# Two groups' weighted sums in one block on TensorE, and three units in another order, in a two-layer cross-attention kernel

## The chip, the cores and the metric

The kernel runs on one core of a Trainium2 chip. The metric is the device time in microseconds (us) from launch to end. A profile of one execution is read beside it; its times count from the start of its own span. TensorE (PE) multiplies and transposes, and loads weights (PEld) under running matmuls; VectorE (DVE), ScalarE (ACT) and GpSimd (POOL) work on what it leaves; SyncE (SP) issues most transfers.

## The reference

For each of 16 images `x` is 112 x 320 and its context 375 x 192. Two cross-attentions follow each other, the first with 8 heads of 40 over 371 context rows, with a small second attention over 4 token rows, the other with 20 heads of 16 over all 375 rows. Cut to what matters:

```python
hs = _mha(x @ Wq, enc @ Wk, enc @ Wv)                 # layer 0, 8 heads
ca_hs1 = _mha((ca.T @ Wq_ca)[:, indices, :], x, x)    # over the image's own 112 rows
ca_hs2 = _mha(ca_hs1 @ Wq, ca @ Wk_ca, ca @ Wv_ca)    # over 4 token rows
x1 = (hs + ca_hs2) @ Wout + b_out + x
q, k, v = heads(x1 @ Wq), heads(ctx @ Wk), heads(ctx @ Wv)   # layer 1, 20 heads
probs = softmax(q @ k.T / 4)
out = (probs @ v) @ Wo + bo + x1
```

## The kernel before

**Groups and iterations.** Heads are worked in groups of four: two groups per image in the first layer (layer 0), five in the second (layer 1). The program is a software pipeline of 18 iterations `t`, each of 7 slots `i`. In slots 0 and 1 the two layer-0 groups of image `t` are scored, in slots 2 to 6 the five layer-1 groups of image `t - 1`. (The last image's are one slot sooner.) In each slot TensorE, in this order, does: the first pair of heads' scores of this slot's group, units, the *shifted scores* of the group of two slots ago (scores again, keys on partitions, with the row maximum as one more row of the product), the transpose of the maxima of the group of one slot ago, units, the second pair's scores, units, the *attend* (probabilities times values) of the group of two slots ago, units. The four places for units are the phases 0 to 3 of `UNITS`, a table written by hand; beside each name stands the image's offset to `t`.

**Units.** K0, K1, V0, V1 are parts of the keys and values; q0 and q1 the queries; q0T and q1T their transposes; W2, S2_0, S2_1, T2_0, T2_1, PV2, S3, p3T the small attentions; N0, N1a, N1b transpose attend results back, and VectorE divides them by the sum of the probabilities (a reciprocal and a product); hn0T, hn1T, x1T transpose the inputs of the projections, out0 and out1 are the projections. All units take two PSUM banks, `bankX0` and `bankX1`, strictly in turn: a unit waits until the unit two places before it has been read out (`bank_drained`). For K0, K1, q0, q1 and the transposes of queries that is ScalarE's rounded copy and then VectorE's remainder or masked copy.

**Queues.** Each engine runs its own list in program order, slot by slot. ScalarE in a slot: phase 0 units, the exponentials of the group of two slots ago (`exps`), the DMA that places the maxima (`place_m`), phase 1, 2, 3 units. VectorE: the first pair's maximum, phase 0 units, the copy of the transposed maxima (`copy_mT`), phase 1 units, the second pair's maximum, phase 2 units, the copy of the attend's result (`copy_o`), phase 3 units.

**Banks.** `bankS` (two banks, one for each head of a pair) holds scores until VectorE has their maximum; `bankST` the shifted scores; `bankO` the attend results and, in its first columns, the transposed maxima `bank_mT`. So before the change a transpose of maxima waits until the attend result has been copied (`o_copied`), and an attend until the maxima have (`mT_copied`). An attend is 12 matmuls: layer 1 puts four heads on four column groups of 32, layer 0 two heads on two column groups of 64. The trace counts each of these fp32 matmuls twice.

Of the kernel before, what the change touches and what calls it, by code (L numbers as in the profile page):

```python
# [11 lines left out]
B, SQ, HID = 16, 112, 320  # L12
SK, CAD, NTOK = 375, 192, 4
# [71 lines left out]
GROUPS = list(SCORED.values())  # L85
NUMBER = {g: n for n, g in enumerate(GROUPS)}


# [23 lines left out]
def xattn_kernel(nc, xT, xpad, ctxT, caS, caT, w_all, w_ca, wqT, bd96, consts, bias, out):  # L112
    g_rows = nc.dram_tensor("g_rows", [B, 3, 32, HID], F32, kind="Internal").ap()

    with ExitStack() as ctx:
# [436 lines left out]
        def _(act):  # L552
# [46 lines left out]
            def unit(name, b):  # L599
# [27 lines left out]
                elif kind == "V0":  # L627
                    if i == 0 and b == 0:
                        act.wait_ge(zeroed, 3)
                    elif i == 0:  # L630
                        act.wait_ge(pv_done, NUMBER[0, b - 1, 1] + 1)
                    nc.scalar.activation(v0[0:KC, i, :].rearrange("p (h d) -> p h d", h=H0)[:, :, 0:D0],
                                         X[0:KC, 0:HID].rearrange("p (h d) -> p h d", h=H0), ACT.Copy)\
                        .then_inc(free, 1)
                elif kind == "V1":
                    if i == 0 and b < 2:
                        act.wait_ge(zeroed, 6 + b)
                    elif i == 0:
                        act.wait_ge(pv_done, NUMBER[1, b - 2, G1 - 1] + 1)
                    nc.scalar.activation(v1[b % 2][0:KC, i, :].rearrange("p (h d) -> p h d", h=H1)[:, :, 0:D1],  # L640
# [90 lines left out]
        def _(dve):  # L731
# [48 lines left out]

            def copy_o(g):
                layer, b, k = g
                n = NUMBER[g]
                dve.wait_ge(pv_done, n + 1)
                if layer == 0:
                    dst, src = o0T[:, 2 * k:2 * k + 2, :].rearrange("p c q -> p (c q)"), bankO[:, 0:2 * SQ]
                else:
                    at = (2 + n % 2) * SQ
                    dst, src = o1T[:, k, :], bankO[:, at:at + SQ]
                nc.vector.tensor_copy(dst, src).then_inc(o_copied, 1)  # L790
# [119 lines left out]
            for t in ITERATIONS:  # L910
                for i in range(SLOTS):
                    g, before, late = scored_at(t, i), scored_at(t, i, 1), scored_at(t, i, LAG)
                    if g:
# [13 lines left out]
                    for u in units_of(t, i, 2):  # L927
                        unit(*u)
                    if late:
                        copy_o(late)  # L930
                    for u in units_of(t, i, 3):
# [14 lines left out]
        def _(pe):  # L946
# [61 lines left out]
            def unit(name, b):  # L1008
# [80 lines left out]
                elif kind in ("N0", "N1a", "N1b"):  # L1089
                    layer, k = {"N0": (0, 1), "N1a": (1, 3), "N1b": (1, 4)}[kind]  # L1090
                    pe.wait_ge(o_copied, NUMBER[layer, b, k] + 1)
                    cols = [o0T[:, c, :] for c in range(4)] if layer == 0 else [
# [43 lines left out]

            def scores(g, pair):
                layer, b, k = g
# [59 lines left out]

            def attend(g, transposed):
                layer, b, k = g  # L1200
                n = NUMBER[g]
                pe.wait_ge(exp_done, n + 1)
                pe.wait_ge(mT_copied, transposed)
                if n > 0:
                    pe.wait_ge(o_copied, n)
                if k == 0:
                    for i in range(NKC):
                        pe.wait_ge(bank_drained[bank(f"V{layer}_{i}", b)], drained(f"V{layer}_{i}", b))
                src = PT[:, n % 2]
                if layer == 0:  # L1210
                    at_once = [(c, j) for pair in range(2) for c in range(NKC) for j in (2 * pair, 2 * pair + 1)]
                else:
                    at_once = [(c, j) for c in range(NKC) for j in range(GROUP)]
                for c, j in at_once:
                    h = GROUP * k + j
                    if layer == 0:
                        keys = KC if c < 2 else KC - NTOK
                        dst = bankO[64 * (j % 2):64 * (j % 2) + 64, (j // 2) * SQ:(j // 2 + 1) * SQ]
                        v = v0[0:keys, c, 64 * h:64 * h + 64]
                    else:  # L1220
                        keys = KC
                        at = (2 + n % 2) * SQ
                        dst = bankO[32 * j:32 * j + 32, at:at + SQ]
                        v = v1[b % 2][0:keys, c, 32 * h:32 * h + 32]
                    last = nc.tensor.matmul(dst, v, src[0:keys, c, SQ * j:SQ * j + SQ], start=(c == 0),  # L1225
                                            stop=(c == NKC - 1))
                last.then_inc(pv_done, 1)
# [16 lines left out]

            attended = transposed = 0
            for t in ITERATIONS:
                for i in range(SLOTS):
                    g, before, late = scored_at(t, i), scored_at(t, i, 1), scored_at(t, i, LAG)
                    if g:
                        scores(g, 0)  # L1250
                    for u in units_of(t, i, 0):
                        unit(*u)
                    if late:
                        shifted_scores(late)
                    if before:
                        transpose_m(before, attended)
                        transposed = NUMBER[before] + 1
                    for u in units_of(t, i, 1):
                        unit(*u)
                    if g:  # L1260
                        scores(g, 1)
                    for u in units_of(t, i, 2):
                        unit(*u)
                    if late:
# [79 lines left out]
```

## Time and profile before

| | before |
|---|---|
| median of three runs | 755.55 us (755.02 to 756.1) |
| profiled execution's own time | 753.38 us |
| its span | 751.5 us |
| TensorE matmul, busy | 703.0 us (94%) |
| TensorE weight load, busy | 610.3 us (81%) |
| VectorE, busy | 472.3 us (63%) |
| ScalarE, busy | 404.0 us (54%) |
| GpSimd, busy | 295.5 us (39%) |
| mean granted TensorE clock | 0.983 |

"Busy" is the union of an engine's instructions. A record `[0.33 <-ACT arena L595]` behind a row of the timeline says that the engine sat idle 0.33 us before it, and which work ended that. The chain of work that ended last follows, back from the end, what released each step; 69% of it is TensorE's. Names such as `L1225` are lines of the kernel: L1159 and L1156 are scores, L1193 and L1187 shifted scores, L1172 the transpose of maxima, L1225 the attend, L1095 the transposes of N0, N1a and N1b, L1111 the S2 units, L1105 W2, L1071 and L1078 query transposes, L1087 the transposes hn0T, hn1T and x1T, L1005 keys, values, queries and projections.

### The profile page before, as it was taken

What the parts mean: (1) busy time and instruction counts of PE and PEld (TensorE: products, weight loads), DVE (VectorE), ACT (ScalarE), POOL (GpSimd) and SP (SyncE); (2) the same over time, 40 slices, a digit from 0 to 9 for tenths busy, and PEclk for the clock granted to TensorE, in tenths of its full rate; (3) what the DMA queues carried; (4) which work ended last, traced back from release to release, by engine and by line L of the source; (5) the groups of instructions that cost most, each with busy time, mean ns of one, the idle gap of its engine ahead of it and who ended that gap; (6) DMA issues with size and microseconds to landing.
All of it is one profiled execution on the core that took longest, in us unless ns stands there. A gap on an engine that the chain in (4) does not pass through costs nothing.

```text
span 751.5 us, 18194 instructions
## 1 busy us (share of the span) xinstructions
PE 703.0 (94%) x6924; PEld 610.3 (81%) x6924; DVE 472.3 (63%) x1028; ACT 404.0 (54%) x923; POOL 295.5 (39%) x401
## 2 busy tenths in 40 slices
PE   8787999999999999999999999999999999999975
PEld 5586888888888888888888888888888888888763
DVE  2653666657576665757576575756667575766662
ACT  2454555555565555565555555556555555654432
POOL 5485662444334253433325344323524542330300
PEclk9889999999999999999999999999999999999996
DMA  9533553443516244252524434261533425051400
GB/s 325 175 96 96 112 133 75 107 80 79 133 47 143 62 119 95 67 118 54 137 60 125 92 80 103 62 142 45 136 81 94 89 76 129 20 137 28 87 7 11
DMA packets 52387, 72.45 MB, mean 96 GB/s; under 512 B 12128, under 2 KB 44256, under 8 KB 52304
## 3 DMA queue, kind: packets, MB, share of 16 engines
q1 hardware_dynamic: 44832, 60.34, 31.7%
q0 software_dynamic: 6144, 9.25, 6.5%
q10 hardware_dynamic: 1328, 1.71, 0.6%
q8 instruction: 57, 0.93, 0.5%
q14 instruction: 26, 0.21, 0.1%
HBM read 20.60 MB, written 4.26 MB: 33 GB/s over the span
## 4 chain that ended last, share of the span: by engine, by line
PE 69%; ACT 13%; DVE 8%; issue 3%; POOL 1%; DMA 1%; SPq 1%; ACTq 0%; POOLq 0%
PE bankX L1005 28%; PE bankO L1225 8%; PE bankST L1193 7%; ACT arena L577 7%; PE bankS L1159 6%; PE bankST L1187 5%; ACT arena L595 3%; DVE negmax L773 2%; DVE q1T L829 2%; PE bankX L1118 2%; PE bankX L1125 2%; PE bankX L1087 2%; PE bankS L1156 2%; ACT q1T L666 2%; PE bankX L1071 2%
## 5 line engine op out<-in xcount | busy, mean ns | idle before, releaser
L773 DVE TENSOR_REDUCE negmax<-bankS 112x2 f32<-112x750 f32 (+1 forms) x224 | 208.7, 932 | 57.0 <-PE bankS L1159 32.7
L494 POOL DMA_DIRECT2D k_stack<-stage x192 | 96.6, 511 | 181.5 <-DVE stage L809 153.9
L577 ACT ACTIVATE arena<-bankST 125x1344 f32<-125x1344 f32 x80 | 103.5, 1294 | 30.9 <-PE bankST L1193 30.9
L1225 PE MATMUL bankO<-arena,v 125*32 125x112 f32 (+2 forms) x2688 | 107.2, 264 | 6.2 <-ACT arena L577 4.4
L1225 PEld LDWEIGHTS bankO<-arena,v 125*32 125x32 f32 (+2 forms) x2688 | 81.2, 117 | 29.0 <-issue 12.7
L1159 PE MATMUL bankS<-k_stack,q1T 112*112 112x376 f32 x320 | 87.8, 355 | 4.1 <-DVE negmax L773 3.0
L1005 PE MATMUL bankX<-ctx_hi,WH 128*120 128x376 f32 (+2 forms) x192 | 69.0, 360 | 3.0 <-DVE qn L765 2.2
L457 POOL TENSOR_TENSOR w2bd<-w2s,cst 96x896 fp32r<-96x896 f32 x16 | 29.9, 1870 | 98.4 <-DVE w2s L765 98.4
L1005 PE MATMUL bankX<-WH,ctx_hi 128*125 128x320 f32 x192 | 66.1, 344 | 0.1
L1193 PE MATMUL bankST<-q1T,k_stack 112*125 112x224 f32 x480 | 65.4, 272 | 0.0
L1005 PE MATMUL bankX<-ctx_hi,WL 128*120 128x376 f32 (+2 forms) x192 | 64.0, 334 | 0.0
L1193 PEld LDWEIGHTS bankST<-q1T,k_stack 112*125 112x125 f32 x480 | 62.0, 188 | 0.8 <-DMA q1T<-mT 0.4
L1005 PE MATMUL bankX<-WL,ctx_hi 128*125 128x320 f32 x192 | 58.5, 312 | 0.0
L1159 PEld LDWEIGHTS bankS<-k_stack,q1T 112*112 112x112 f32 x320 | 49.4, 177 | 8.8 <-DVE negmax L773 6.5
L829 DVE TENSOR_SCALAR q1T<-bankX,odd_rows 128x448 fp32r<-128x448 f32 (+1 forms) x48 | 29.1, 606 | 41.7 <-ACT q1T L666 41.2
L595 ACT ACTIVATE arena<-bankX,negmax 112x112 f32<-112x112 f32 x128 | 43.6, 354 | 21.7 <-DVE negmax L837 21.6
L1005 PE MATMUL bankX<-WH,act_hi 128*112 128x320 f32 x144 | 46.7, 325 | 3.3 <-DVE act_hi L866 1.4
L483 POOL TENSOR_TENSOR xb<-xp,bias_sb 112x320 f32<-112x320 f32 x16 | 13.9, 867 | 88.7 <-DVE x L860 88.6
L779 DVE CAST mT<-bankO 4x112 fp32r<-4x112 f32 x112 | 29.0, 259 | 30.0 <-PE bankO L1172 30.0
L1187 PEld LDWEIGHTS bankST<-q0T,k_stack 121*125 121x125 f32 (+1 forms) x384 | 46.0, 187 | 0.0
L619 ACT ACTIVATE stage<-bankX 128x376 fp32r<-128x376 f32 (+1 forms) x48 | 23.1, 482 | 41.7 <-PE bankX L1005 41.0
L1187 PE MATMUL bankST<-q0T,k_stack 121*125 121x112 f32 (+1 forms) x384 | 44.9, 266 | 0.0
(141 smaller groups left out, 1545.8 us busy)
## 6 DMA issues: line engine op xcount, KB each, us to landing
k_stack<-stage SPq DMA_DIRECT2D x96, 176.2 KB
k_stack<-stage SPq DMA_DIRECT2D x192, 70.5 KB, 2.6
k_stack<-stage POOLq DMA_DIRECT2D x192, 47.0 KB, 2.0
ctx_raw<-in_ctxT SPq DMA_DIRECT2D x16, 376.0 KB, 3.3
k_stack<-stage SPq DMA_DIRECT2D x48, 117.5 KB
xp<-in_xpad SPq DMA_DIRECT2D x16, 224.0 KB, 3.3
x_raw<-in_xT SPq DMA_DIRECT2D x16, 168.0 KB, 2.4
out<-x1b SPq DMA_DIRECT2D x16, 140.0 KB, 3.2
```

The costliest lines, as they stand in the source:

```text
L457: nc.gpsimd.tensor_tensor(w2bd[:, :, :], w2s[:, :].bitcast(F32).unsqueeze(1).broadcast_to((96, H0, SQ)), mask96.unsqueeze(2).broadcast_to( ...
L494: pool.dma_start(dst, src).then_inc(k1_stacked_pool[b % 2], 16)
L577: nc.scalar.activation(dst[0:KC], bankST[0:KC, :, 0:GROUP * SQ], ACT.Exp).then_inc(exp_done, 1)
L595: last = nc.scalar.activation(prob2[0:SQ, h, :], X[0:SQ, (h % 4) * SQ:(h % 4 + 1) * SQ], ACT.Exp, bias=negmax2[:, h:h + 1], accum_out=sum2 ...
L773: nc.vector.tensor_reduce(negmax[:, n % 2, 2 * pair:2 * pair + 2], bankS[0:SQ, :, 0:keys], axis=AX, op=ALU.max, negate=True).then_inc(max_ ...
L779: nc.vector.tensor_copy(mT[:, n % MT_BUFS, :], bank_mT).then_inc(mT_copied, 1)
L829: nc.vector.tensor_scalar(q1T[:, 4 * i:4 * i + g, 1, :], X[:, 0:g * SQ].rearrange("p (h q) -> p h q", h=g), odd_rows[:, :], None, ALU.mult ...
L1005: last = nc.tensor.matmul(dst, lhs, rhs, start=(n == 0), stop=(n == len(passes) - 1))
L1159: last = nc.tensor.matmul(bankS[0:SQ, j, 0:SKP], q1T[0:ROWS1, h // 2, h % 2, :], k1_stack[b % 2][0:ROWS1, h // 2, :], start=True, stop=True)
L1187: last = nc.tensor.matmul(bankST[0:keys, c, SQ * j:SQ * j + SQ], k0_stack[0:M_ROW0 + 1, h, KC * c:KC * c + keys], q0T[0:M_ROW0 + 1, h, :], ...
L1193: last = nc.tensor.matmul(bankST[0:KC, c, 2 * SQ * pair:2 * SQ * pair + 2 * SQ], k1_stack[b % 2][0:ROWS1, 2 * k + pair, KC * c:KC * c + KC ...
L1225: last = nc.tensor.matmul(dst, v, src[0:keys, c, SQ * j:SQ * j + SQ], start=(c == 0), stop=(c == NKC - 1))
```

## The change

Attends are done by *episodes*: the two layer-0 groups in one block, in the slot of the second (slot 3), the layer-1 groups 0 and 1 in slot 5, 2 and 3 in slot 0 of the next iteration, and 4 alone in slot 1. The other slots (2, 4, 6) have no attend. `pv_done` and `o_copied` count episodes. The transposed maxima move from `bankO` to free columns of the second bank of `bankS`; their transpose now waits for the first maximum of this slot's group, since VectorE reads that bank, and the second head's scores wait until the maxima are copied. In the table, N1a ("four groups' transposes") moves from slot 1 phase 3 to phase 1, between q1T_2 and q0; in slot 4 out1 moves to phase 1, and p3T and N0 to phase 2.

```diff
-    ([("q1T_1", -1), ("V1_2", -1)], [("q1T_2", -1)], [("q0", 1)], [("N1a", -2), ("K1_0", 0)]),
+    ([("q1T_1", -1), ("V1_2", -1)], [("q1T_2", -1), ("N1a", -2)], [("q0", 1)], [("K1_0", 0)]),
...
-    ([("K0_2", 1)], [("p3T", 0), ("N0", 0)], [("out1", -2)], [("q0T_0", 1)]),
+    ([("K0_2", 1)], [("out1", -2)], [("p3T", 0), ("N0", 0)], [("q0T_0", 1)]),
...
+EPISODES = [e for b in range(B + 1) for e in
+            ([[(0, b, 0), (0, b, 1)]] if b < B else []) +
+            ([[(1, b - 1, 0), (1, b - 1, 1)], [(1, b - 1, 2), (1, b - 1, 3)], [(1, b - 1, 4)]] if b > 0 else [])]
+EPISODE = {g: n for n, e in enumerate(EPISODES) for g in e}
+def attended_at(t, i):
+    late = scored_at(t, i, LAG)
+    return EPISODES[EPISODE[late]] if late and EPISODES[EPISODE[late]][-1] == late else None
...
-        bank_mT = bankO[0:GROUP, 0:SQ]
+        bank_mT = bankS[0:GROUP, 1, SKP + 8:SKP + 8 + SQ]
...
-                    act.wait_ge(pv_done, n - 1)
+                    act.wait_ge(pv_done, EPISODE[GROUPS[n - 2]] + 1)
...
                 for j in range(2):
                     h = GROUP * k + 2 * pair + j
+                    if j == 1 and transposed > 0:
+                        pe.wait_ge(mT_copied, transposed)
...
-            def transpose_m(g, attended):
+            def transpose_m(g, scoring):
                 n = NUMBER[g]
-                pe.wait_ge(max_done, 2 * n + 2)
+                if scoring:
+                    pe.wait_ge(max_done, 2 * NUMBER[scoring] + 1)
+                else:
+                    pe.wait_ge(max_done, 2 * n + 2)
                 if n > 0:
                     pe.wait_ge(mT_copied, n)
-                else:
-                    pe.wait_ge(g_split, 4)
-                if attended > 0:
-                    pe.wait_ge(o_copied, attended)
...
-            def attend(g, transposed):
+            def attend(groups):
+                n = EPISODE[groups[0]]
                 if n > 0:
                     pe.wait_ge(o_copied, n)
+                for g in groups:
+                    layer, b, k = g
+                    pe.wait_ge(exp_done, NUMBER[g] + 1)
...
-                    if late:
-                        attend(late, transposed)
-                        attended = NUMBER[late] + 1
+                    if attended_at(t, i):
+                        attend(attended_at(t, i))
```

VectorE's `copy_o` copies an episode at once (448 columns in layer 0, 224 or 112 in layer 1), in `attended_at`'s slots.

The rows below are TensorE's list in a middle iteration. First slot 1, before: q1T_2's second transpose, the second pair's scores, the first and last of q0's eight matmuls, the attend of group 4, N1a (`o1T`) and the first matmul of K1_0.

```order
L1078 MATMUL bankX<-cst,qn 128x112
L1156 MATMUL bankS<-k_stack,q0T 112x372 [waits max_done]
L1156 MATMUL bankS<-k_stack,q0T 112x372
L1005 MATMUL bankX<-WH,x_hi 112x320 [waits x_split,bank_drained1]
...
L1225 MATMUL bankO<-arena,v_1 32x112 [waits o_copied,mT_copied,exp_done]
L1225 MATMUL bankO<-arena,v_1 32x112 x11
L1095 MATMUL bankX<-cst,o1T 112x128 [waits o_copied,bank_drained0]
L1095 MATMUL bankX<-cst,o1T 112x128 x3
L1005 MATMUL bankX<-ctx_hi,WH 128x376 [waits bank_drained1]
```

The same place of the changed kernel:

```order
L1090 MATMUL bankX<-cst,qn 128x112
L1107 MATMUL bankX<-cst,o1T 112x128 [waits o_copied,bank_drained1]
L1107 MATMUL bankX<-cst,o1T 112x128 x3
L1170 MATMUL bankS<-k_stack,q0T 112x372 [waits max_done]
L1170 MATMUL bankS<-k_stack,q0T 112x372 [waits mT_copied]
L1017 MATMUL bankX<-WH,x_hi 112x320 [waits x_split,bank_drained0]
...
L1241 MATMUL bankO<-arena,v_1 32x112 [waits exp_done,o_copied]
L1241 MATMUL bankO<-arena,v_1 32x112 x11
L1017 MATMUL bankX<-ctx_hi,WH 128x376 [waits bank_drained1]
```

N1a has gone ahead of the scores, and q0 has changed banks: it follows q1T_2 in bank 0, where it followed V1_2 in bank 1.

Slot 2, before, from S2_0 (`w2bd`) to S2_1, with N1b and the attend of layer 0's first group between:

```order
L1111 MATMUL bankX<-w2bd,ca_st 112x448 [waits w2_expanded,ca_split,bank_drained0]
L1159 MATMUL bankS<-k_stack,q1T 112x376 [waits max_done]
L1159 MATMUL bankS<-k_stack,q1T 112x376
L1095 MATMUL bankX<-cst,o1T 112x128 [waits o_copied,bank_drained1]
L1225 MATMUL bankO<-arena,v 64x112 [waits bank_drained0,bank_drained1,o_copied,mT_copied,exp_done]
L1225 MATMUL bankO<-arena,v 64x112 x11
L1111 MATMUL bankX<-w2bd,ca_st 112x448 [waits bank_drained0]
```

The same place of the changed kernel:

```order
L1123 MATMUL bankX<-w2bd,ca_st 112x448 [waits w2_expanded,ca_split,bank_drained0]
L1173 MATMUL bankS<-k_stack,q1T 112x376 [waits max_done]
L1173 MATMUL bankS<-k_stack,q1T 112x376 [waits mT_copied]
L1107 MATMUL bankX<-cst,o1T 112x128 [waits o_copied,bank_drained1]
L1123 MATMUL bankX<-w2bd,ca_st 112x448 [waits bank_drained0]
```

The attend is gone from between the two S2 halves, which share a bank; its twelve matmuls stand in slot 3 now.

Slot 4 of the changed kernel, from the transpose of the maxima to hn0T of slot 5 (before, p3T and N0 stood behind the transpose, and out1 and an attend behind the second pair's scores):

```order
L1185 MATMUL bankS<-cst,negmax 4x112 [waits mT_copied,max_done]
L1017 MATMUL bankX<-WH,act_hi 112x320 [waits bank_drained1,bank_drained0]
...
L1173 MATMUL bankS<-k_stack,q1T 112x376 [waits max_done]
L1173 MATMUL bankS<-k_stack,q1T 112x376 [waits mT_copied]
L1110 MATMUL bankX<-cst,p3w 96x112 [waits p3_split,bank_drained1]
L1107 MATMUL bankX<-cst,o0T 112x128 [waits o_copied,bank_drained0]
L1107 MATMUL bankX<-cst,o0T 112x128 x3
L1083 MATMUL bankX<-cst,qn 120x112 [waits bank_drained0,bank_drained1]
...
L1099 MATMUL bankX<-cst,hn 128x112 [waits bank_drained0]
```

N0 now takes the bank of out1, two places before it, and only q0T_0 and the next slot's scores stand between N0 and hn0T.

## Rows read from the trace of the kernel before

**Rows 1.** The page's granted TensorE clock, in 40 slices of the span.

```profile
PEclk9889999999999999999999999999999999999996
```

**Rows 2.** Timeline, slot 1: start us, duration us, engine, line, operation [idle before].

```profile
337.62 1.29 ACT L577 ACTIVATE arena<-bankST 125x1344 f32<-125x1344 f32 x1 [0.21 <-PE bankST L1193]
...
337.72 0.57 PE L1156 MATMUL bankS<-k_stack,q0T 120*112 120x372 f32 x2
...
338.13 0.31 PE L1005 MATMUL bankX<-WH,x_hi 128*112 128x320 f32 x1
...
338.81 0.34 ACT L666 ACTIVATE q1T<-bankX 64x224 fp32r<-64x224 f32 x1
...
339.18 0.45 DVE L829 TENSOR_SCALAR q1T<-bankX,odd_rows 128x224 fp32r<-128x224 f32 x1 [1.21 <-ACT q1T L666]
...
340.93 0.45 PE L1005 MATMUL bankX<-ctx_hi,WH 128*128 128x376 f32 x1 [0.17 <-DVE qn L765]
...
341.90 0.51 PE L1159 MATMUL bankS<-k_stack,q1T 112*112 112x376 f32 x2
```

**Rows 3.** Timeline, slots 2 and 3, and S2_1 one iteration later.

```profile
345.17 0.44 PE L1111 MATMUL bankX<-w2bd,ca_st 96*112 96x448 f32 x1
...
347.86 0.46 PE L1111 MATMUL bankX<-w2bd,ca_st 96*112 96x448 f32 x1 [0.33 <-ACT arena L595]
...
352.28 1.38 PE L1225 MATMUL bankO<-arena,v 125*64 125x112 f32 x24
...
353.59 0.43 PE L1005 MATMUL bankX<-ctx_hi,WH 128*120 128x376 f32 x1
...
391.19 0.46 PE L1111 MATMUL bankX<-w2bd,ca_st 96*112 96x448 f32 x1 [0.29 <-ACT arena L595]
```

**Rows 4.** The chain that ended last: start us, us on the chain, what.

```profile
346.35 1.46 ACT arena L595 x8
...
369.83 1.17 PE bankX L1005 x8
371.00 0.71 PE bankO L1225 x24
```

**Rows 5.** Timeline, slots 4 and 5.

```profile
355.83 0.93 DVE L773 TENSOR_REDUCE negmax<-bankS 112x2 f32<-112x750 f32 x1
...
356.42 0.26 PE L1172 MATMUL bankO<-cst,negmax 112*4 112x112 f32 x1
...
357.27 0.65 PE L1095 MATMUL bankX<-cst,o0T 128*112 128x128 f32 x4 [0.49 <-DVE stage L814]
...
357.96 0.21 DVE L795 RECIPROCAL r<-bankX 112x8 f32<-112x8 f32 x1 [0.46 <-PE bankX L1095]
...
358.20 0.49 DVE L797 TENSOR_TENSOR hn<-bankX,r 112x320 f32<-112x320 f32 x1
...
359.83 0.49 DVE L872 TENSOR_TENSOR x1b<-bankX,x1b 112x320 f32<-112x320 f32 x1 [0.29 <-PE bankX L1005]
...
362.51 0.81 PE L1193 MATMUL bankST<-q1T,k_stack 112*125 112x224 f32 x6
```

**Rows 6.** Timeline, slots 5, 6 and 0.

```profile
363.46 0.26 DVE L779 CAST mT<-bankO 4x112 fp32r<-4x112 f32 x1 [0.52 <-PE bankO L1172]
...
370.93 0.54 PEld L1225 LDWEIGHTS bankO<-arena,v 125*32 125x32 f32 x24 [0.20 <-issue]
...
371.77 0.49 DVE L765 SCALAR_TENSOR_TENSOR qn<-bankX,qn 112x320 fp32r<-112x320 f32 x1 [0.97 <-ACT qn L653]
...
372.82 0.31 PE L1005 MATMUL bankX<-WH,ctx_hi 128*125 128x320 f32 x1
...
376.89 0.82 PE L1105 MATMUL bankX<-x_raw,bd 128*96 128x112 f32 x6 [0.25 <-DVE q1T L829]
```

**Rows 7.** Timeline near the end, slot 3 of the last image.

```profile
724.84 0.94 DVE L773 TENSOR_REDUCE negmax<-bankS 112x2 f32<-112x750 f32 x1 [0.34 <-PE bankS L1159]
...
725.29 0.26 PE L1172 MATMUL bankO<-cst,negmax 112*4 112x112 f32 x1
```

More of the change, by code:

```diff
@@ L630, in unit @@
                     elif i == 0:
-                        act.wait_ge(pv_done, NUMBER[0, b - 1, 1] + 1)
+                        act.wait_ge(pv_done, EPISODE[0, b - 1, 1] + 1)
                     nc.scalar.activation(v0[0:KC, i, :].rearrange("p (h d) -> p h d", h=H0)[:, :, 0:D0],
@@ L779, in copy_mT, with copy_o @@
                 nc.vector.tensor_copy(mT[:, n % MT_BUFS, :], bank_mT).then_inc(mT_copied, 1)
[L781 to L784, printed above, removed]
+            def copy_o(groups):
+                layer, b, k = groups[0]
+                dve.wait_ge(pv_done, EPISODE[groups[0]] + 1)
                 if layer == 0:
-                    dst, src = o0T[:, 2 * k:2 * k + 2, :].rearrange("p c q -> p (c q)"), bankO[:, 0:2 * SQ]
+                    dst, src = o0T[:, :, :], bankO[:, 0:4 * SQ]
                 else:
-                    at = (2 + n % 2) * SQ
-                    dst, src = o1T[:, k, :], bankO[:, at:at + SQ]
+                    dst, src = o1T[:, k:k + len(groups), :], bankO[:, 2 * SQ:(2 + len(groups)) * SQ]
+                dst = dst.rearrange("p c q -> p (c q)")
                 nc.vector.tensor_copy(dst, src).then_inc(o_copied, 1)
@@ L911, in _ @@
                 for i in range(SLOTS):
-                    g, before, late = scored_at(t, i), scored_at(t, i, 1), scored_at(t, i, LAG)
+                    g, before = scored_at(t, i), scored_at(t, i, 1)
                     if g:
@@ L928, in _ @@
                         unit(*u)
-                    if late:
-                        copy_o(late)
+                    if attended_at(t, i):
+                        copy_o(attended_at(t, i))
                     for u in units_of(t, i, 3):
@@ L1090, in unit @@
                     layer, k = {"N0": (0, 1), "N1a": (1, 3), "N1b": (1, 4)}[kind]
-                    pe.wait_ge(o_copied, NUMBER[layer, b, k] + 1)
+                    pe.wait_ge(o_copied, EPISODE[layer, b, k] + 1)
                     cols = [o0T[:, c, :] for c in range(4)] if layer == 0 else [
@@ L1135, in unit, with scores @@
                 last.then_inc(unit_filled, 1)
-            def scores(g, pair):
+            def scores(g, pair, transposed):
                 layer, b, k = g
@@ L1197, in shifted_scores @@
                 last.then_inc(st_done, 1)
-            def attend(g, transposed):
[L1200 to L1203, printed above, removed]
+            def attend(groups):
+                n = EPISODE[groups[0]]
                 if n > 0:
                     pe.wait_ge(o_copied, n)
[L1206 to L1211, printed above, removed]
-                else:
-                    at_once = [(c, j) for c in range(NKC) for j in range(GROUP)]
-                for c, j in at_once:
-                    h = GROUP * k + j
+                else:
+                    pe.wait_ge(g_split, 4)
+                for g in groups:
+                    layer, b, k = g
+                    pe.wait_ge(exp_done, NUMBER[g] + 1)
+                    if k == 0:
+                        for i in range(NKC):
+                            pe.wait_ge(bank_drained[bank(f"V{layer}_{i}", b)], drained(f"V{layer}_{i}", b))
+                    src = PT[:, NUMBER[g] % 2]
@@ L1225, in attend @@
-                    last = nc.tensor.matmul(dst, v, src[0:keys, c, SQ * j:SQ * j + SQ], start=(c == 0),
-                                            stop=(c == NKC - 1))
+                        at_once = [(c, j) for pair in range(2) for c in range(NKC) for j in (2 * pair, 2 * pair + 1)]
+                    else:
+                        at_once = [(c, j) for c in range(NKC) for j in range(GROUP)]
+                    for c, j in at_once:
+                        h = GROUP * k + j
+                        if layer == 0:
+                            keys = KC if c < 2 else KC - NTOK
+                            at = (2 * k + j // 2) * SQ
+                            dst = bankO[64 * (j % 2):64 * (j % 2) + 64, at:at + SQ]
+                            v = v0[0:keys, c, 64 * h:64 * h + 64]
+                        else:
+                            keys = KC
+                            at = (2 + k % 2) * SQ
+                            dst = bankO[32 * j:32 * j + 32, at:at + SQ]
+                            v = v1[b % 2][0:keys, c, 32 * h:32 * h + 32]
+                        last = nc.tensor.matmul(dst, v, src[0:keys, c, SQ * j:SQ * j + SQ], start=(c == 0),
+                                                stop=(c == NKC - 1))
@@ L1243, in _ @@
             unit("S2_1", 0)
-            attended = transposed = 0
+            transposed = 0
             for t in ITERATIONS:
@@ L1249, in _ @@
                     if g:
-                        scores(g, 0)
+                        scores(g, 0, transposed)
                     for u in units_of(t, i, 0):
@@ L1255, in _ @@
                     if before:
-                        transpose_m(before, attended)
+                        transpose_m(before, g)
                         transposed = NUMBER[before] + 1
@@ L1260, in _ @@
                     if g:
-                        scores(g, 1)
+                        scores(g, 1, transposed)
                     for u in units_of(t, i, 2):
                         unit(*u)
-                    if late:
-                        attend(late, transposed)
-                        attended = NUMBER[late] + 1
+                    if attended_at(t, i):
+                        attend(attended_at(t, i))
                     for u in units_of(t, i, 3):
```

9 lines of the change are left out of this document (1 added, 8 removed).

## The prediction

> **What bounds the kernel now.** I read the busy shares and the granted clock first, then the timeline of one steady iteration (slot 1 at 335 us to slot 0 at 377 us), then the chain of waits through it. TensorE holds the chain nearly everywhere, and its clock is at full speed from 45 us to 740 us [rows 1]. So a change matters by what it does to TensorE's own order: work taken out, and units that come before what they wait for is ready. Every iteration is the same: the second S2 half starts at 347.86 us and one iteration later at 391.19 us [rows 3], so an iteration is 43.3 us.
>
> TensorE stands still in four places of it. The S2 half waits 0.33 us for ScalarE's exponentials of the other half [rows 3, 4]; K1_0 waits for VectorE's q0 remainder [rows 2]; N0 waits 0.49 us for VectorE's K0 remainder [rows 5]; W2 waits 0.25 us for q1T_0's masked copy [rows 6].
>
> **The change, part by part.**
>
> *The switch.* An attend of the second layer, four narrow tiles side by side in six waves, costs more than its waves: the load queue is idle 0.20 us ahead of it [rows 6], and it holds TensorE for 0.71 us [rows 4]. Its 24 loads begin within 0.54 less 0.11 us [rows 6], so a wave is a little under 0.10 us, and 0.14 us of the 0.71 us are no work. With some 0.09 us of standstill ahead and 0.05 us in the next unit's second matmul I estimate 0.28 us for each attend's two switches. The change joins three pairs of attends per iteration and so has 0.84 us to gain, over 16 images 13.4 us. The Trainium skill, "TensorEngine Tiling (Array Packing)", section Key Properties, states that changing the tiling mode drains TensorE; by it alone fewer changes can only help, and the time would be that of the first rival below. The trace shows the idle time that it speaks of.
>
> But a joined pair also takes the first attend out of its own slot (2, 4 and 6), where it may have lain over a wait. I go through the slots.
>
> *Slot 1: N1a between q1T_2 and q0.* Units take the two banks in turn, so q0 now gets the bank of q1T_2 instead of V1_2's. That bank is free only when ScalarE, which first does the exponentials of 1.29 us from 337.62 us, has copied it (338.81 us, 0.34 us) and VectorE has masked it (339.18 us, 0.45 us), at 339.63 us [rows 2]. A release takes 0.05 us (346.35 + 1.46 to 347.86 us, rows 4 and 3), so q0 starts at 339.68 us, where it started at 338.13 us [rows 2]. Only N1a, some 0.40 us, is new ahead of it, so TensorE stands still for some 1.1 us. From there on follow q0's eight matmuls (1.17 us [rows 4], and 0.10 us more, since after a standstill the second load is not ahead), 0.09 us and 0.71 us for the attend [rows 4], and K1_0, which took 341.90 - 340.93 = 0.97 us to the next slot's scores [rows 2] and no longer waits: 339.68 + 0.10 + 1.17 + 0.80 + 0.97 = 342.72 us against 341.90 us, **+0.82 us**. Bounds: 0, if the exponentials were not ahead of that copy, and +1.1 us, if K1_0's wait stayed.
>
> *Slots 2 and 3: the first layer's pair.* The first S2 half is on TensorE at 345.17 us; VectorE's maximum and ScalarE's eight records of 1.46 us from 346.35 us end at 347.81 us, and the second half starts at 347.86 us [rows 3, 4]. No attend is in this chain, so removing the attend from slot 2 moves nothing: TensorE waits from some 346.1 us on, where it worked. The attend's twelve waves then stand in slot 3, where nothing waits: there an attend takes 353.59 - 352.28 = 1.31 us, and its second half adds 1.38 us less 0.26 us of one result and plus one first step, 1.17 us [rows 3]. **+1.17 us**. Bounds: +1.0 us, if the chain is 0.15 us sooner with VectorE's copy gone, and 1.3 us.
>
> *Slots 4 and 5.* Before, from the transpose of the maxima (356.42 us) to the shifted scores of slot 5 (362.51 us) there are N0's wait and an attend [rows 5]. After: the transpose writes into the scores' bank and so waits for this slot's first maximum, which ends at 355.83 + 0.93 = 356.76 us [rows 5]: it starts at 356.82 us, +0.40 us. out1 follows at once (eight matmuls in 1.17 us [rows 4]) to 358.09 us, the scores to 358.43 us, p3T to 358.53 us. N0 needs out1's bank: its last result at 358.25 us, VectorE's addition of 0.49 us [rows 5], N0 at 358.83 us, a wait of 0.3 us. On VectorE the maximum of the scores comes next (0.93 us, to 359.73 us), then N0's reciprocal of 0.21 us and product of 0.49 us [rows 5], with releases to 360.49 us. hn0T can start at 360.54 us; TensorE, with q0T_0 and the scores, is there some 0.4 us earlier. V0_0 then has no wait, and with 0.34 us for hn0T's transposes and 5/8 of 1.17 us for V0_0 the shifted scores start at 360.54 + 0.34 + 0.73 = 361.61 us: 0.90 us sooner than 362.51 us. Of this 0.58 us is the attend's waves, which come back in slot 5, and 0.05 us the wait below. **-0.27 us**; bounds -0.9 us (no wait at N0 and hn0T) and +0.2 us.
>
> *Slots 6 and 0.* Without the attend (0.71 us, its switch and the exposed load) V0_2 starts 0.92 us earlier, but V1_0, two units on, needs q1's bank, which VectorE gives up at 371.77 + 0.49 = 372.26 us [rows 6]. It starts at 372.31 us and not 372.82 us, and with the exposed load that is 0.40 us won. The waves come back as 0.58 us in slot 0, where they lie over W2's wait (0.25 us in the row, 0.32 us with the load) [rows 6]. With two of the waits below, **-0.04 us**.
>
> *The maxima's copy.* Each second scores matmul now waits for VectorE's copy of the transposed maxima (0.26 us at 363.46 us [rows 6]). It ends at 363.72 us, and the second load stood at some 363.65 us. I take 0.05 us in the slots 0, 3, 5 and 6, 0 to 0.13 us; three are in the sums above, one is left: **+0.05 us**. Elsewhere out1, N1a or S3 cover it. Fewer and larger copies on VectorE (busy 63%) cost nothing, since no chain above starts from one.
>
> *Sum.* 0.82 + 1.17 - 0.27 - 0.04 + 0.05 = 1.73 us per iteration. All units are there in iterations 2 to 14, 13 times: 22.5 us. In iterations 0 and 1 the S2 chain bounds in the same way, but slot 3's attend waited for its exponentials, which the first half now fills: about +1.2 us for both. In the last two nothing fills the slots, and the transpose of the maxima waits for this slot's maximum: the maximum at 724.84 us ends at 725.78 us, the transpose stood at 725.29 us [rows 7], so +0.5 us in each of four or five slots, less an attend's switches: +2 us. Together +25.7 us on the profiled execution's own 753.38 us: 779.1 us. That execution is 2.2 us under the median of the three runs (755.55 us), which would give 781.3 us; I say 780 us.
>
> **Rivals.**
>
> 1. *The cover is not needed.* The switches are saved everywhere (13.4 us), N0's and W2's waits go (0.49 us and 0.25 us, 14 times, 10 us), and the waits of q0 and S2 do not come: 755.55 - 23.4 = 732 us. For it speaks that 0.84 us of every iteration are plainly idle. For a mere gain the two new waits would have to stay under some 0.6 us of their 2.0 us together; that would need ScalarE to reach q1T_2's copy before the exponentials, against its program order, or S2's eight records to start before VectorE's maximum ends. Chance 0.08, and 0.03 that both sides cancel (756 us).
> 2. *Only one large wait comes.* Without the q0 term the sum is 13 x 0.82 = 10.7 us less, 769 us; without the S2 term 15 us less, 765 us. The second is the weaker rival, since the chain's own rows [rows 3, 4] give both of its ends. Chance 0.17.
> 3. *The clock falls.* At the end, after a few microseconds in which TensorE mostly waits, its level goes from 2.4 GHz to 1.2 GHz [rows 1]. The new standstills are 1.7 us and 1.1 us an iteration. If one fall of 13 us, as near the start, came in every second iteration, it would add some 6 us each: over 820 us. Against it: the level holds through the last two iterations up to the 39th slice, though TensorE has little to fill its waits there. Chance 0.04.
>
> **How the numbers follow.** The forecast has 0.68: 773 to 788 us, by the bounds of slots 1 and 4. With rival 2 down to 764 us that is 0.85, so the range is 764 to 788 us. A difference of 0.2% (1.5 us) is about what can be told from none. Slower: 0.68 + 0.17 + 0.04 = 0.89; faster 0.08; same 0.03.
>
> **What would show it.** In the profile after: an iteration of 45.0 us; q0's first matmul idle behind VectorE's q1T in some 13 iterations, about 14 us in total; the second S2 half idle behind ScalarE's exponentials for some 1.6 us each instead of 0.3 us; the transpose of the maxima idle behind VectorE's maximum in slot 4; N0 idle behind out1's addition instead of K0's remainder; attends of 48 records in 1.4 us (second layer) and 2.5 us (first). The prediction is wrong if the S2 half starts sooner after its sister than 2.7 us, or if q0 does not wait for q1T_2.

## The result, and the profile after

| | before | after |
|---|---|---|
| median of four runs each | 755.83 us (755.02 to 759.11) | 830.76 us (825.88 to 838.34) |
| ratio, 95% interval | | 1.0962 (1.091 to 1.1014) |
| span of the profiled execution | 751.5 us | 836.5 us |
| mean granted TensorE clock in it | 0.983 | 0.903 |

The kernel is 9.6% slower. The direction was forecast, but 830.8 us lies far outside 764 to 788 us. The profiled execution is the longest of the four (838.34 us) and counts as a slow run, which the ratio leaves out; the two shortest, 825.88 and 826.19 us, have a clock of 0.921, so sums below, made on its span, run some 8 us above the median.

The page after: busy time, then the granted clock in 40 slices, beside the one of [rows 1].

```profile
PE 758.7 (91%) x6924; PEld 666.8 (80%) x6924; DVE 467.4 (56%) x980; ACT 405.7 (48%) x923; POOL 294.6 (35%) x401
...
PEclk7879899798989989998999989899998989898966
```

TensorE has the same 6924 records, but its busy time rose from 703.0 to 758.7 us: the same work took longer. The clock line says why: it is not at full speed in the middle any more. Two iterations cut into stretches show it: us, busy time of PE, PEld, DVE, ACT and POOL with the records in brackets, granted clock, DMA share, GB/s.

```profile
387.50:394.30 6.80, 6.80 (x42) 6.36 (x42) 3.65 (x8) 3.79 (x13) 4.30 (x9) 0.50 0.27 48
394.30:435.30 41.00, 37.63 (x390) 33.42 (x387) 24.30 (x52) 20.68 (x43) 12.79 (x16) 1.00 0.37 91
435.30:442.10 6.80, 6.80 (x37) 6.36 (x37) 3.58 (x8) 4.08 (x15) 3.92 (x8) 0.50 0.23 46
442.10:483.10 41.00, 37.61 (x394) 33.40 (x391) 24.32 (x52) 20.49 (x42) 13.18 (x17) 1.00 0.38 92
483.10:489.90 6.80, 6.80 (x33) 6.36 (x33) 3.26 (x9) 4.14 (x15) 3.03 (x6) 0.50 0.21 38
```

For 6.8 us the clock is 0.50, that is 1.2 GHz; for the 41 us between it is 2.4 GHz. It falls in all twelve steady iterations: in nine for 6.8 us, in two for 3.4 us and in the first for 10.2 us. In the stretches shown at 1.2 GHz TensorE is busy throughout. What stands ahead of them is in the waits of TensorE: line, what it waited for, us in total, times, longest.

```profile
PE bankX L1123 <- ACT arena L608: 22.0, 13, 1.7
PE bankX L1017 <- DVE q1T L841: 12.4, 13, 1.0
PE bankS L1185 <- DVE negmax L786: 7.8, 18, 2.4
...
PE bankS L1173 <- DVE mT L792: 1.5, 4, 0.7
```

L1123 is S2_1, L1017 q0 (among others), L1185 the transpose of the maxima, L1173 scores. The first was 4.2 us in 13 times before, the second and third are new. Both forecast standstills are there, 13 times each, and the timeline has them in their places:

```profile
424.46 0.45 DVE L841 TENSOR_SCALAR q1T<-bankX,odd_rows 128x224 fp32r<-128x224 f32 x1 [1.20 <-ACT q1T L679]
424.96 0.40 PE L1017 MATMUL bankX<-WH,x_hi 128*112 128x320 f32 x1 [0.95 <-DVE q1T L841]
...
426.32 0.78 PE L1241 MATMUL bankO<-arena,v 125*32 125x112 f32 x24
...
427.99 0.51 PE L1173 MATMUL bankS<-k_stack,q1T 112*112 112x376 f32 x2
...
431.25 0.44 PE L1123 MATMUL bankX<-w2bd,ca_st 96*112 96x448 f32 x1
...
433.67 0.21 ACT L608 ACTIVATION_READ_ACCUMULATOR arena<-bankX,negmax 112x1 f32 x1
433.94 0.46 PE L1123 MATMUL bankX<-w2bd,ca_st 96*112 96x448 f32 x1 [1.69 <-ACT arena L608]
...
435.56 2.58 PE L1200 MATMUL bankST<-q0T,k_stack 121*125 121x112 f32 x12
...
439.70 0.83 PE L1173 MATMUL bankS<-k_stack,q1T 112*112 112x376 f32 x2
...
441.01 3.04 PE L1241 MATMUL bankO<-arena,v 125*64 125x112 f32 x48
```

The two S2 halves are 433.94 - 431.25 = 2.69 us apart, as in [rows 3], and the standstill between them grew from 0.33 to 1.69 us, since the attend that filled it is gone (e3 below puts it back). Some 1.4 us after it ends the clock falls. Slot 3's twelve shifted scores then take 2.58 us (1.40 us at 429.20 us, at full speed), the scores 0.83 us instead of 0.51 us. The chain that ended last has the same: start us, us on the chain, what.

```profile
429.36 1.24 PE bankST L1200 x12
...
432.44 1.46 ACT arena L608 x8
...
435.76 2.37 PE bankST L1200 x12
...
441.08 2.97 PE bankO L1241 x48
```

The same twelve matmuls, for two groups of layer 0, cost 1.24 us at one level and 2.37 us at the other, a few microseconds apart.

### The profile page after: what moved, and what is told of

It reads as the page before. It is cut to its first block, busy times and chain, and to the rows that moved or that the text cites. A ratio compares the mean times of both kernels' runs of the same rounds, so it can differ in the third digit from the quotient of the medians.

```text
span 836.5 us, 18066 instructions
## 1 busy us (share of the span) xinstructions
PE 758.7 (91%) x6924; PEld 666.8 (80%) x6924; DVE 467.4 (56%) x980; ACT 405.7 (48%) x923; POOL 294.6 (35%) x401
## 4 chain that ended last, share of the span: by engine, by line
PE 73%; DVE 10%; ACT 7%; issue 2%; POOL 1%; DMA 1%; SPq 1%; ACTq 0%; POOLq 0%
PE bankX L1017 28%; PE bankO L1241 12%; PE bankST L1200 7%; PE bankS L1173 6%; PE bankST L1206 5%; DVE negmax L786 3%; ACT arena L608 2%; PE bankX L1099 2%; ACT arena L590 2%; PE bankX L1130 2%; PE bankX L1137 2%; PE bankS L1170 2%; PE bankS L1185 1%; PE bankX L1090 1%; PE bankX L1145 1%
## 5 line engine op out<-in xcount | busy, mean ns | idle before, releaser
L1241 PEld LDWEIGHTS bankO<-arena,v 125*32 125x32 f32 (+2 forms) x2688 | 90.4, 125 | 18.2 <-issue 17.4
L1173 PE MATMUL bankS<-k_stack,q1T 112*112 112x376 f32 x320 | 97.5, 384 | 6.9 <-DVE negmax L786 4.9
L1017 PE MATMUL bankX<-ctx_hi,WH 128*120 128x376 f32 (+2 forms) x192 | 78.6, 410 | 1.7 <-ACT arena L608 1.7
L1017 PE MATMUL bankX<-ctx_hi,WL 128*120 128x376 f32 (+2 forms) x192 | 74.3, 387 | 0.0
L1173 PEld LDWEIGHTS bankS<-k_stack,q1T 112*112 112x112 f32 x320 | 57.2, 191 | 15.0 <-DVE negmax L786 8.0
L1017 PE MATMUL bankX<-WH,ctx_hi 128*125 128x320 f32 x192 | 65.9, 343 | 2.9 <-DVE qn L778 2.9
L1200 PEld LDWEIGHTS bankST<-q0T,k_stack 121*125 121x125 f32 (+1 forms) x384 | 64.8, 253 | 0.0
L1200 PE MATMUL bankST<-q0T,k_stack 121*125 121x112 f32 (+1 forms) x384 | 62.3, 328 | 0.0
L638 ACT ACTIVATE stage<-bankX 120x376 fp32r<-120x376 f32 (+1 forms) x48 | 23.2, 484 | 76.3 <-PE bankX L1017 76.3
L792 DVE CAST mT<-bankS 4x112 fp32r<-4x112 f32 x112 | 29.2, 261 | 52.4 <-PE bankS L1185 52.4
L1017 PE MATMUL bankX<-WL,ctx_hi 128*125 128x320 f32 x192 | 58.2, 310 | 0.0
L826 DVE TENSOR_TENSOR stage<-bankX,stage 120x376 fp32r<-120x376 f32 (+1 forms) x48 | 26.2, 545 | 49.1 <-ACT stage L638 49.1
L1017 PE MATMUL bankX<-WH,act_hi 128*112 128x320 f32 x144 | 46.9, 325 | 1.4 <-DVE act_hi L878 1.4
```

The source lines that it names most:

```text
L792: nc.vector.tensor_copy(mT[:, n % MT_BUFS, :], bank_mT).then_inc(mT_copied, 1)
L1017: last = nc.tensor.matmul(dst, lhs, rhs, start=(n == 0), stop=(n == len(passes) - 1))
L1200: last = nc.tensor.matmul(bankST[0:keys, c, SQ * j:SQ * j + SQ], k0_stack[0:M_ROW0 + 1, h, KC * c:KC * c + keys], q0T[0:M_ROW0 + 1, h, :], ...
```

## The experiments

Ratios are to the runs of before on the same chip; the medians of before that ran beside them are 755.53 us (e1 to e4), 754.68 us (e5 to e8) and 755.47 us (e9, e10). For every kernel I compare, besides the time, three parts of the profiled span: the head (to the first S2 half of image 3), the mean length of an iteration (that half of image 3 to that of image 15, by 12), and the tail (from there to the end). The halves' rows are those of L1123 (L1111 before) in the timeline.

| kernel | median us (runs) | ratio (95%) | iteration | head | tail | clock |
|---|---|---|---|---|---|---|
| before | 755.55 (3) | | 43.32 | 128.60 | 103.14 | 0.983 |
| after | 830.76 (4) | 1.0962 (1.091 to 1.1014) | 47.93 | 143.09 | 118.26 | 0.903 |
| e1, S2 filled | 791.02 (4) | 1.0454 (1.0406 to 1.0503) | 45.01 | 135.49 | 108.96 | 0.975 |
| e10, q0 filled | 827.61 (4) | 1.1006 (1.0935 to 1.1078) | 47.82 | 137.76 | 113.76 | 0.923 |
| e2, N1a back | 793.54 (4) | 1.048 (1.0429 to 1.0532) | 45.34 | 137.42 | 110.11 | 0.944 |
| e3, layer 0 single | 765.02 (4) | 1.0118 (1.0081 to 1.0155) | 43.80 | 129.96 | 107.81 | 0.979 |
| e4, both | 756.29 (12) | 0.9992 (0.9966 to 1.0018) | 43.01 | 128.82 | 107.87 | 0.977 |
| e5, layer-0 pair, maxima | 823.24 (4) | 1.0884 (1.0837 to 1.0931) | 47.12 | 143.01 | 111.10 | 0.924 |
| e6, maxima alone | 761.63 (6) | 1.0076 (1.005 to 1.0103) | 43.49 | 129.13 | 109.05 | 0.977 |
| e9, layer-1 pairs alone | 751.45 (12) | 0.9945 (0.9913 to 0.9978) | 42.90 | 129.40 | 102.06 | 0.985 |
| e7, e9 and slot 4's order | 742.09 (6) | 0.9835 (0.9795 to 0.9874) | 42.35 | 128.46 | 106.03 | 0.973 |
| e8, e7 with N1a first | 746.09 (6) | 0.9878 (0.9834 to 0.9921) | 42.50 | 128.93 | 105.55 | 0.975 |

**Theory:** the standstill of 1.7 us between the S2 halves, without the attend that lay in it, is what brings the clock down; the waits themselves cost what was forecast. **Rivals:** q0's standstill (or the two together) does it; or the order as a whole keeps TensorE waiting, and the clock is a small part.

### Filling the standstill (e1)

```diff
+            def fill(count):
+                for _ in range(count):
+                    nc.tensor.matmul(bankO[:, 448:512], ident[:, :], cst[:, 0:64], start=True, stop=True)
...
+                    if i == 2 and 1 < t < B - 1:
+                        fill(9)
```

> The changed kernel plus nine extra 128x64 transposing matmuls into unused columns of bankO behind N1b in slot 2 of iterations 2 to 14, where TensorE stands still for 1.7 us until ScalarE has done the first S2 half; their result is not read. Theory (the standstill costs twice: itself, and a fall of the clock to 1.2 GHz right behind it, some 3.1 us per iteration): the clock stays at 2.4 GHz in the steady iterations, the iteration falls from 47.8 us to some 44.7 us and the time from 826-838 us to 775-790 us, though the kernel does more work. Rival (the time is all waits of the new order, the clock only mirrors an idle TensorE): no gain, 826-838 us. Rival (the 1.0 us wait of q0 triggers the fall by itself): no gain either, and the low stretches begin in slot 1.

Measured: 791.0 us, 40 us less than the changed kernel, with 9 matmuls more in each of 13 iterations. The iteration is 45.01 us, 1.69 us over the kernel before. The fill between the S2 halves in its timeline, then 45 us, one iteration, in the columns of the stretches above:

```profile
405.58 0.44 PE L1123 MATMUL bankX<-w2bd,ca_st 96*112 96x448 f32 x1
...
406.41 2.12 PE L1247 MATMUL bankO<-cst 128*128 128x64 f32 x18
408.34 0.43 PE L1123 MATMUL bankX<-w2bd,ca_st 96*112 96x448 f32 x1
```

```profile
425.00:470.00 45.00, 43.28 (x446) 38.90 (x446) 28.09 (x61) 24.64 (x58) 17.14 (x24) 1.00 0.39 91
```

S2_1 still comes 2.76 us after its sister: the fill wins no time there. It wins 2.9 us per iteration behind it, because the clock stays at 1.00. This separates the price of the clock from that of the waits. The median missed the expected 775 to 790 us by 1 us: head and tail, which the fill doesn't reach, stay long.

### One standstill at a time (e2, e3, e10)

e2 puts N1a back, so that q0 gets its old bank; S2's standstill stays:

```diff
-    ([("q1T_1", -1), ("V1_2", -1)], [("q1T_2", -1), ("N1a", -2)], [("q0", 1)], [("K1_0", 0)]),
+    ([("q1T_1", -1), ("V1_2", -1)], [("q1T_2", -1)], [("q0", 1)], [("N1a", -2), ("K1_0", 0)]),
```

> The changed kernel with N1a back in phase 3 of slot 1, so that q0 again takes the bank of V1_2. The wait of q0 behind q1T_2's masked copy (some 1.0 us, 12.4 us in all in the profile) should be gone, 0.82 us per iteration. If the S2 standstill alone makes the clock fall, low stretches stay in each iteration and the time is 11 us under the changed kernel, 815-825 us. If it takes both standstills, the clock stays up and the time is 763-772 us.

e3 attends layer 0's groups one at a time (with their copies); q0's standstill stays:

```diff
-            ([[(0, b, 0), (0, b, 1)]] if b < B else []) +
+            ([[(0, b, 0)], [(0, b, 1)]] if b < B else []) +
```

> The changed kernel with the first layer's two groups attended one by one again, in slots 2 and 3; the second layer's stay paired. The first attend lies over the S2 wait again: its idle time falls from 1.7 us to some 0.3 us per iteration and slot 3's attend is 1.17 us shorter. If the S2 standstill causes the falls of the clock, the clock is at 2.4 GHz throughout and the time 755-763 us. If q0's wait is enough, low stretches stay and the time is above 790 us.

e10 leaves everything of the changed kernel and fills q0's standstill instead of S2's:

```diff
+                    if i == 1 and 1 < t < B - 1:
+                        fill(6)
```

> The changed kernel plus six extra 128x64 matmuls ahead of q0 in slot 1, over its wait of 1.0 us; the S2 standstill of 1.7 us is left as it is. Their result is not read. Theory (the S2 standstill is enough for the fall): low stretches stay in most iterations and the time is 815-838 us. Rival (q0's standstill helps to bring the clock down): most falls go and the time is 780-800 us, as with the S2 standstill filled.

The waits of e3 and the clock of e3, e10 and e2, in this order:

```profile
PE bankX L1017 <- DVE q1T L841: 12.5, 13, 1.0
...
PE bankX L1123 <- ACT arena L608: 4.9, 13, 0.4
```

```profile
PEclk9889999999999999999999999999999999999977
```

```profile
PEclk9779899998999999898999989899998989899978
```

```profile
PEclk9779899997999999999988999998999999999985
```

e3 has q0's standstill in full and no fall in the middle: 765.0 us (2 us over its range) and 43.80 us an iteration. e10 has S2's alone and falls in every iteration (traced in a run of 827.22 us), at 827.6 us, as expected by the theory: filling q0's wait changes almost nothing. So S2's standstill is what the falls need, and q0's is not.

But e2 has S2's standstill too, in full length, and falls in only four of its twelve steady iterations, once briefly:

```profile
PE bankX L1123 <- ACT arena L608: 22.0, 13, 1.7
```

Its iterations last 44.13 to 44.29 us without a fall, 48.32 to 48.42 us with one of 10.2 us and 45.70 us with one of 3.4 us; it came out at 793.5 us, between the two cases that I had named. The standstill is thus needed, but does not decide alone in which iteration the clock falls. e2 and e10 differ in what stands ahead of S2 (N1a's place, q0's bank, six matmuls); which of it decides wasn't found.

What does hold for the changed kernel, e10, e2 and e5 (below) is where a fall begins. They have 38 falls in their steady iterations, and each begins between 1.1 us before and 1.7 us after the start of the second S2 half, that is, inside the standstill or shortly behind it. The four falls that began inside it lasted 10.2 us, all others 6.8 or 3.4 us.

The Trainium skill, "TensorE: Matmul & The Clock Gate", section "A second HAM failure mode: psum-queue depth-cycling", describes a kernel in which TensorE is idle for short times between groups of matmuls, often enough that the clock goes to and fro. The trace agrees in kind only: here it is one idle time of 1.7 us in some 48 us.

### Both back, and the maxima's bank (e4, e5, e6)

e4 has both edits above. e5 keeps of the change the layer-0 pair and the maxima's new bank alone: `UNITS` as before, and layer 1 one group at a time (with its copies), as below. e6 has e3's edit too, so that the new bank alone is left.

```diff
-            ([[(1, b - 1, 0), (1, b - 1, 1)], [(1, b - 1, 2), (1, b - 1, 3)], [(1, b - 1, 4)]] if b > 0 else [])]
+            ([[(1, b - 1, 0)], [(1, b - 1, 1)], [(1, b - 1, 2)], [(1, b - 1, 3)], [(1, b - 1, 4)]] if b > 0 else [])]
```

> The changed kernel with both taken back: first-layer groups attended one by one, N1a in phase 3 of slot 1. What is left of the change is the second layer's pairs, the transposed maxima in the scores' bank, and out1 ahead of p3T and N0. By my sum without its two large terms, and with 0.35 us per iteration more won in slot 4 than I had summed, the iteration is some 42.7 us and the time 745-751 us: faster than the kernel before (755.8). Rival (the new waits on the maxima eat what the saved switches give): 754-760 us.

> Only the first layer's pair of the change, with the transposed maxima in the scores' bank (which a pair of 448 columns needs); the second layer's groups one by one, the order of units as before. Theory: the S2 standstill of 1.7 us is there, q0's is not; an iteration without a fall is some 44.5 us (43.3 + 1.17), and the clock falls in some iterations but not in all, as in the run with N1a back: 785-800 us. If a standstill near 1.7 us never makes it fall without the rest of the change, 770-775 us.

> Only the new place of the transposed maxima and its two waits (this slot's first maximum, the copy ahead of the second scores matmul); no pairs, order of units as before. Theory: in the steady iterations the 0.4 us wait in slot 4 lies over N0's old wait, so an iteration stays within 43.3 to 43.5 us; in the last two iterations, where nothing fills the slots, the maxima chain grows and the stretch from the last image's S2 half to the end goes from 103.1 us to some 107 us. Time 758-762 us. If the tail's loss comes from the pairs, the stretch stays at 103 us and the time within 1 us of the kernel before.

e4 is back at the time of before (756.3 us), in the range of its rival: its iterations are 0.31 us shorter, as the prediction's sum had it (for this run I had expected 0.6 us), but its tail is 4.7 us longer. e5 shows the clock again: its iteration is 44.60 to 44.63 us where the clock holds and 47.76 to 47.80 us where it falls (46.20 us once, with a short fall), which is in ten of twelve, more often than I expected; 823.2 us, not 785 to 800. e6 met its range. An iteration is 0.17 us longer by the new bank, and the tail 5.9 us. Its waits have one that is new:

```profile
PE bankS L1185 <- DVE negmax L786: 7.7, 18, 2.3
```

The transpose of the maxima waits for a maximum of the group being scored: 0.25 us in slot 4 of each iteration, 2.3 us once in the head, and 2.0 us together in the tail, where few units fill a slot. That is at most a third of the tail's 5.9 us. The clock also falls sooner at the end, and the tail has 22.0 us at 1.2 GHz, against 11.3 us before. Of one stretch of the tail, before and in e6:

```profile
710.00:740.00 30.00, 22.90 (x282) 17.72 (x280) 16.53 (x35) 12.34 (x16) 0.00 (x0) 1.00 0.07 14
```

```profile
710.00:740.00 30.00, 25.78 (x256) 20.51 (x256) 17.30 (x35) 10.56 (x16) 0.87 (x1) 0.83 0.13 21
```

How the rest of the 5.9 us is shared between other waits and this earlier fall was not tested.

### What is worth keeping (e9, e7, e8)

e9 has only layer 1's pairs, with the maxima in `bankO` and the waits of before. e7 has slot 4's new order as well. e8 puts N1a ahead of q1T_2, so that q0 gets N1a's bank and not q1T_2's. All three have e4's edits and this one (with the waits and places of before that go with it):

```diff
-        bank_mT = bankS[0:GROUP, 1, SKP + 8:SKP + 8 + SQ]
+        bank_mT = bankO[0:GROUP, 0:SQ]
```

e9 has this line besides; the pair below it is e8's alone:

```diff
-    ([("K0_2", 1)], [("out1", -2)], [("p3T", 0), ("N0", 0)], [("q0T_0", 1)]),
+    ([("K0_2", 1)], [("p3T", 0), ("N0", 0)], [("out1", -2)], [("q0T_0", 1)]),
```

```diff
-    ([("q1T_1", -1), ("V1_2", -1)], [("q1T_2", -1)], [("q0", 1)], [("N1a", -2), ("K1_0", 0)]),
+    ([("q1T_1", -1), ("V1_2", -1)], [("N1a", -2), ("q1T_2", -1)], [("q0", 1)], [("K1_0", 0)]),
```

> As the kernel with second-layer pairs and the old place of the maxima (742.1 us, an iteration of 42.35 us), but slot 4's units in the order of before (p3T and N0 in phase 1, out1 in phase 2). It tells the two parts of that gain of 0.97 us per iteration apart. Theory: two pairs save two attends' switches, 0.56 us by my estimate, less q1's wait in slot 0: an iteration of 42.8 to 43.1 us and 748-752 us; the rest is out1's order. Rival: the pairs alone give all of it, 742 us.

> The kernel before with two parts of the change: the second layer's groups in pairs, and out1 ahead of p3T and N0. The transposed maxima stay in bankO with the old waits; the first layer's groups stay single, N1a stays in phase 3. Theory: steady iterations gain the 0.3 us seen with the maxima in the scores' bank plus what the new waits cost there (0.05 us in four slots, up to 0.4 us in slot 4): 42.3 to 42.8 us; the last stretch stays near 103 us. Time 744-750 us, faster than the kernel before. Rival: hn0T's wait behind the maximum and N0 in slot 4 takes all of it, 753-757 us.

> As the kernel with second-layer pairs and the old place of the maxima, and in slot 1 N1a in phase 1 ahead of q1T_2 (the change put it behind). Then q0 takes N1a's bank, which VectorE frees some 0.7 us after N1a without ScalarE's exponentials before it, and K1_0 takes q1T_2's. Theory: q0 does not stand still as in the change, and K1_0's wait for q0's remainder (some 0.3 us) goes: 0.3 us per iteration under the same kernel with N1a in phase 3, 3-5 us in all. Rival (any unit between q1T_2 and q0's old place delays q0 as in the change): 8-12 us slower than that kernel.

e9 met its range: it takes 0.42 us off an iteration, for two joins of layer 1 (at 0.28 us each the prediction's switches would be 0.56 us). e7 takes off another 0.55 us, and with 742.1 us (I had expected 744 to 750 us) it beats both kernels, 1.65% under the one before. Its tail of 106.03 us is that of one trace, of a run of 744.49 us; though the maxima are in the old bank, it is 2.9 us longer than before, with 25.8 us of it at 1.2 GHz (before 11.3 us). Slot 4, in e4 and in e7: from the last shifted scores to the transpose of the maxima.

```profile
354.49 0.82 PE L1206 MATMUL bankST<-q1T,k_stack 112*125 112x224 f32 x6
354.57 0.93 DVE L786 TENSOR_REDUCE negmax<-bankS 112x2 f32<-112x750 f32 x1
...
355.55 0.26 PE L1185 MATMUL bankS<-cst,negmax 112*4 112x112 f32 x1 [0.25 <-DVE negmax L786]
```

```profile
350.79 0.81 PE L1205 MATMUL bankST<-q1T,k_stack 112*125 112x224 f32 x6
350.86 0.93 DVE L786 TENSOR_REDUCE negmax<-bankS 112x2 f32<-112x750 f32 x1
...
351.44 0.26 PE L1184 MATMUL bankO<-cst,negmax 112*4 112x112 f32 x1
```

The distance is 1.06 us in e4 and 0.65 us in e7: 0.41 us (forecast 0.40 us) of the 0.66 us by which their iterations differ. The rest comes in steps of 0.03 to 0.06 us from one slot's shifted scores to the next, which is what the prediction had for the waits on the maxima's copy. In e7 the transposes of N0 no longer wait for K0's remainder, where before had 7.4 us of it in 15 times; e9 still has it:

```profile
PE bankX L1107 <- DVE stage L826: 7.5, 15, 0.5
```

That is most of the 0.55 us.

e8 failed my theory of a gain, and its rival of a loss of 8 to 12 us. The wait moved:

```profile
PE bankX L1017 <- DVE hn L809: 3.6, 13, 0.3
```

q0 follows N1a in its bank and waits for VectorE's product of it. 42.50 us an iteration and 746.1 us, against 42.35 and 742.1 us: nothing is won by N1a being sooner, and 0.15 us an iteration lost. That is 1.8 us in twelve; the other 2.2 us of the medians lie within the scatter of the runs.

## Why the prediction was right in direction and wrong in size

1. **Slot 1, +0.82 us: right.** q0 stands still 0.95 us, to 424.96 us, 0.05 us after VectorE's masked copy; from there to the next scores it is 3.03 us (forecast 3.04). Taken alone it is e3 less e4: 43.80 - 43.01 = 0.79 us.
2. **Slots 2 and 3, +1.17 us: right as waits go.** S2_1 follows 2.69 us after S2_0, unmoved, and stands still 1.69 us. e2's iterations without a fall (mean of eight) less e4's: 44.17 - 43.01 = 1.16 us.
3. **Slots 4, 5, 6, 0 and the maxima's copy, -0.26 us: right.** e4 less before: -0.31 us. Slot by slot it is right too. Against before, the shifted scores of e4 start 0.95 us sooner in slot 5 (forecast 0.90 us), 0.31 us in slot 6 (0.27 us), 0.65 us in slot 0 (0.67 us) and 0.35 us in slot 1 (0.31 us). N0's load stands behind out1's addition in 14 iterations, 6.2 us in all, and a pair of attends takes 1.36 us in layer 1 (forecast 1.4 us) and 2.54 us in layer 0 in e1 (2.5 us). Behind the -0.31 us stands a gain of 0.42 us from two joined pairs (e9) and of 0.55 us from slot 4 (e7), most of which the maxima's new bank takes back (e4 against e7, 0.66 us). From the transpose of the maxima to slot 5's shifted scores it is 451.94 - 447.21 = 4.73 us after; forecast 4.79, before 6.09 [rows 5]:

```profile
447.21 0.26 PE L1185 MATMUL bankS<-cst,negmax 112*4 112x112 f32 x1 [0.25 <-DVE negmax L786]
...
451.94 0.82 PE L1206 MATMUL bankST<-q1T,k_stack 112*125 112x224 f32 x6
```

4. **The steady sum, +1.73 us per iteration: right**, to 0.04 us, by e1 (1.69 us, 0.07 us of it its fill, which puts the second S2 half at 2.76 us instead of 2.69 us). The three differences above give 1.64 us. Twelve such iterations are 20 us.
5. **The clock: the step that failed.** The sum has it at nothing. It was named as the third rival, with a chance of 0.04, as a fall of 13 us in every second iteration at 6 us. It falls in every one, for 6.8 us in most, and costs 47.93 - 45.01 = 2.92 us on the mean; 35 us in twelve iterations. What I set against it, that the level holds through the last two iterations of before though TensorE has little to do there, did not carry over to this pattern of waits; why not stays open. The size of a standstill told more: the longest of the steady part went from 0.5 to 1.7 us.
6. **Head and tail, +1.2 and +2 us: too small.** The head grew by 14.5 us, the tail by 15.1 us. e1 leaves 6.9 and 5.8 us of them; the other 7.6 and 9.3 us go with 20 and 24 us more at 1.2 GHz. In e1's head the clock falls twice for 10.2 us (before once, 13.7 us), and e3, without the layer-0 pair, has a head of 129.96 us, so most of it comes with the pair. The tail of e1 has 2.0 us of the transpose's waits and an earlier fall of the clock, as e6's; "+0.5 us in each of four or five slots" was right in size for the waits and left out the rest. By itself this term is enough to miss the range: e1, whose clock holds in the steady part, has a median of 791.0 us, and the range ends at 788 us.

On the span: head 14.5, twelve iterations 55.4 (20.4 as waits, 35.0 as clock), tail 15.1, together 836.5 - 751.5 = 85.0 us.

What stays open: why the clock falls in every iteration of the changed kernel and of e10, in ten of twelve of e5 and in four of twelve of e2, at the same standstill.

## What to carry to other kernels

Before taking a unit out of a place, look at what its standstill becomes there: a wait that grows from 0.3 to 1.7 us may cost another 2.9 us through TensorE's clock, and nine matmuls that nobody reads, put into it, took 40 us off. Joining work to save switches paid where no wait of more than 0.2 us came up in the places left empty (layer 1, e9), and cost where one of 1.7 us did (layer 0, e5). When two pieces of a change share a bank or take turns in one, try each alone: here two of its parts made 742 us, and the whole 831 us.

## What the runs showed of the hardware

Busy stretches at 1.2 GHz cost a little under half of their length: 3.1 us of 6.8 us after (iterations of 48.08 us, e1's 45.01 us), 3.2 us of 6.8 us in e5, 4.2 us of 10.2 us in e2. The clock fell after a standstill of 1.7 us that came once in some 48 us, with TensorE busy for 37.6 us of the 41 us ahead of the fall; a standstill of 1.0 us (e3) never did it in the steady part. The same standstill of 1.7 us did it in twelve of twelve iterations of two kernels, in ten of e5's and in four of e2's.
